# Four-layer graph network on one Trainium2 core: extra matmuls into an unused PSUM bank in five loops

## The chip, the cores and the metric

One core of a Trainium2 chip runs the whole program as one launch. The metric is the device time of one execution in microseconds (us); lower is better. PE is TensorE, DVE VectorE, ACT ScalarE, POOL GpSimd, SP SyncE.

## The reference

The graph has 3125 nodes with 128 numbers each and 100,000 edges, sorted by destination. Four layers follow one another, each ending in a residual and a layer norm:

```python
x = layernorm(x + L0(x))   # mean of x[dst] summed at src, then two 128x128 layers with relu
x = layernorm(x + L1(x))   # attention: q[dst] . (k[src] + e), softmax per dst, sum of weighted (v[src] + e), then gelu layers
x = layernorm(x + L2(x))   # (x + 3 * sum over edges of w * x[src_of_edge]) / 4
x = layernorm(x + L3(x))   # 18 relation matrices; messages of both directions summed at dst and at src
```

All numbers are float32.

## The kernel before

Edges are cut into tiles of 128, nodes into 25 blocks of 128. A (tile, block) couple that holds at least one edge of the block is a *pair*; there are 816 pairs, padded. A sum over edges is, for a pair, one 128x128 matmul of a 0/1 matrix ("hot", made by DVE by comparing locations with a row of column numbers) with 128 rows. Five loops matter here. In all of them POOL issues one indirect DMA for each of the 816 pairs, from the software queue.

- `send_rows` (L515 matmul, L501 hot matrix, L530 copy to SBUF, L562 indirect DMA). A step is four pairs; six steps ("ways") make a round, 34 rounds, 204 steps. SP loads the locations, DVE makes the hot matrix, PE multiplies it with rows of `x` that are picked by block number, ACT copies the product, POOL scatters it to DRAM. A way is used again after PE, ACT and the scatter have finished with it.
- `scores` (L1161 transpose, L1165 q matmuls, L1169 edge-feature matmul, L1077 indirect gather, L1122 and L1128 to L1135 on DVE, L1061 index copy). A step is four pairs, four ways, 51 rounds, 204 steps. PE transposes the edge features, ACT copies them, PE makes q (four 128-wide matmuls) and the feature product (one 512-wide one). DVE then adds (L1128), multiplies and reduces. POOL copies the indices of the step after the current one before it gathers the current one, and waits for that step's DVE addition of the round before.
- `gather_sum`, called three times (tags g2, g3, g4; L731 indirect gather, L742 hot matrix, L763 matmuls). A group is eight pairs, six ways, 17 rounds, 102 groups for each call. POOL's instructions are written out, and from the second round on it waits for `summed` of the way; so does DVE before it makes the way's hot matrix. PE waits for the hot matrices and the gathered rows, runs the eight matmuls, which add up in PSUM banks 0 to 6, and the last one increments `summed`.

TensorE's program in each of these loops first reads the block numbers of the step or group into registers, then waits, then runs its matmuls. Bank 7 of PSUM isn't used in them: `gather_sum` holds 25 x 128 columns, `send_rows` banks 0 to 5, `scores` banks 0 to 5. Nothing in them writes `S["ident"]` or the first block rows of `S["x"]`.

Other stages: sorting and tables (to about 523 us), `first_sum` (1724 to 2203), `weigh_values` (3789 to 4227), `messages` (5516 to 5633) and small ones between. They aren't touched.

Of the kernel before, what the change touches and what calls it, by code (L numbers as in the profile page):

```python
# [52 lines left out]
BANK = 512  # L53
# [408 lines left out]
                last.then_inc(turned, 1)  # L462


def send_rows(nc, S, dram):


# [4 lines left out]
    with ExitStack() as stack:  # L472
# [8 lines left out]
        ps = S["ps"]  # L481
        block = stack.enter_context(nc.Block())

        @block.sync
        def _(sp):
            with sp.Fori(0, WHOLE) as i:
                for q in range(WAYS):
                    sp.wait_ge(heated[q], i + 1)
                    sp.dma_start(locb[:, q, :], dram["loc"][bass.ds(i * (WAYS * STEP) + q * STEP, STEP), :]
                                 .rearrange("(a k) e -> a (k e)", a=1).to_broadcast([P, STEP * P])).then_inc(placed[q], 16)  # L490
# [12 lines left out]
        @block.tensor  # L503
        def _(pe):
            for q in range(WAYS):
                pe.sem_inc(picked[q], 1)
            with pe.Fori(0, WHOLE) as i:
                for q in range(WAYS):
                    _, cols = nc.values_load_multi_w_load_instructions(
                        S["dst_steps"][0:1, bass.ds(i * (WAYS * STEP) + q * STEP + PAIR_COLS, STEP)], engines=[mybir.EngineType.PE],  # L510
                        min_val=0, max_val=(BLOCKS - 1) * D, skip_runtime_bounds_check_because="block numbers are counts of blocks")
                    pe.wait_ge(heated[q], i + 2)
                    pe.wait_ge(laid[q], i * 2 + 1)
                    for j in range(STEP):
                        last = pe.matmul(ps[:, q * BANK + j * P:q * BANK + (j + 1) * P], hot_t[:, q, j * P:(j + 1) * P],  # L515
                                         S["x"][:, bass.ds(cols[j], D)], start=True, stop=True)
                    last.then_inc(picked[q], 1)
# [176 lines left out]
def load_columns(nc, S, eng, name, table, start):  # L694

    base = table * PAIR_COLS
    limits = [(BLOCKS - 1) * AW, (BLOCKS - 1) * D, (TILES - 1) * P]
    _, values = nc.values_load_multi_w_load_instructions(
        S[name + "_steps"][0:1, bass.ds(start + base, GROUP)], engines=[eng], min_val=0, max_val=limits[table],
        skip_runtime_bounds_check_because="counts of blocks and tiles, capped when they were made")  # L700
    return values


def gather_sum(nc, S, tag, name, table, index, weight=None, fresh=True):


    width, WAYS = D, 6
    WHOLE = PAIRS_PAD // (WAYS * GROUP)
    with ExitStack() as stack:
        m = Memory(nc, stack)  # L710
        got = m.sb(tag + "_got", [P, WAYS, GROUP, D])
        hot = m.sb(tag + "_hot", [P, WAYS, GROUP, P])
        landed, summed, heated = ([m.sem(f"{tag}_{n}{q}") for q in range(WAYS)] for n in (
            "landed", "summed", "hot"))
        hot_order, cleared = m.sem(tag + "_order"), m.sem(tag + "_cleared")
        loc, ps = S[name + "_loc"], S["ps"]
        block = stack.enter_context(nc.Block())

        def start_of(i, q):
            return i * (WAYS * GROUP) + q * GROUP  # L720

        @block.gpsimd
        def _(pool):
            for i in range(WHOLE):
                for q in range(WAYS):
                    if i:
                        pool.wait_ge(summed[q], i + 1)
                        pool.nop(nofuse=True)
                    for j in range(GROUP):
                        c = i * (WAYS * GROUP) + q * GROUP + j  # L730
                        pool.indirect_dma_start(out=got[:, q, j, :], out_offset=None, in_=table,  # L731
                                                in_offset=bass.IndirectOffsetOnAxis(ap=index[:, c:c + 1], axis=0)).then_inc(landed[q], 16)

        @block.vector
        def _(dve):
            if fresh:
                dve.memset(ps[:, 0:BLOCKS * D], 0.0).then_inc(cleared, 1)
            with dve.Fori(0, WHOLE) as i:
                for q in range(WAYS):
                    start = start_of(i, q)  # L740
                    dve.wait_ge(summed[q], i + 1)
                    one = dve.tensor_tensor(hot[:, q], S["col"][:, :].unsqueeze(1).to_broadcast([P, GROUP, P]),  # L742
                                            loc[:, bass.ds(start, GROUP)].unsqueeze(2).to_broadcast([P, GROUP, P]), ALU.is_equal)
                    if weight is not None:
                        one.then_inc(hot_order, 1)
                        dve.wait_ge(hot_order, i * WAYS + q + 1)
                        one = dve.tensor_tensor(hot[:, q], hot[:, q],
                                                weight[:, bass.ds(start, GROUP)].unsqueeze(2).to_broadcast([P, GROUP, P]), ALU.mult)
                    one.then_inc(heated[q], 1)

        @block.tensor
        def _(pe):
            for q in range(WAYS):
                pe.sem_inc(summed[q], 1)
            if fresh:
                pe.wait_ge(cleared, 1)
            with pe.Fori(0, WHOLE) as i:
                for q in range(WAYS):
                    columns = load_columns(nc, S, mybir.EngineType.PE, name, 1, start_of(i, q))
                    pe.wait_ge(heated[q], i + 1)  # L760
                    pe.wait_ge(landed[q], (i + 1) * (16 * GROUP))
                    for j in range(GROUP):
                        last = pe.matmul(ps[:, bass.ds(columns[j], width)], hot[:, q, j, :], got[:, q, j, 0:width],  # L763
                                         start=False, stop=True, skip_group_check=True)
                    last.then_inc(summed[q], 1)
            for q in range(WAYS):
                pe.wait_ge(summed[q], WHOLE + 1)
# [250 lines left out]
def scores(nc, S, dram):  # L1018
# [6 lines left out]
    with ExitStack() as stack:  # L1025
# [13 lines left out]
        ps = S["ps"]  # L1039
        block = stack.enter_context(nc.Block())  # L1040

        def qe(q):
            return ps[:, (q % 2) * 2 * BANK:(q % 2) * 2 * BANK + STEP * D]

        def feat(q):
            return ps[:, (q % 2) * 2 * BANK + BANK:(q % 2) * 2 * BANK + BANK + STEP * D]

        def turn(q):
            return ps[:, (4 + q % 2) * BANK:(4 + q % 2) * BANK + P]

        def before_last(eng, sems, q, i):

            if q < 2:
                eng.wait_ge(sems[q + 2], i + 1)
            else:
                eng.wait_ge(sems[q - 2], i + 2)
# [91 lines left out]
        @block.tensor  # L1148
        def _(pe):
            for q in range(WAYS):  # L1150
                pe.sem_inc(turned[q], 1)
                pe.sem_inc(product[q], 1)
            with pe.Fori(0, WHOLE) as i:
                for q in range(WAYS):
                    start = i * (WAYS * STEP) + q * STEP
                    _, cols = nc.values_load_multi_w_load_instructions(
                        S["dst_steps"][0:1, bass.ds(start + PAIR_COLS, STEP)], engines=[mybir.EngineType.PE], min_val=0,
                        max_val=(BLOCKS - 1) * D, skip_runtime_bounds_check_because="block numbers are counts of blocks")
                    pe.wait_ge(featured[q], (i + 1) * (16 * STEP))
                    before_last(pe, kept, q, i)  # L1160
                    pe.transpose(turn(q), attr[:, q, :], S["ident"][:, :]).then_inc(turned[q], 1)  # L1161
                    before_last(pe, scored, q, i)
                    pe.wait_ge(heated[q], i + 2)
                    for j in range(STEP):
                        pe.matmul(qe(q)[:, j * D:(j + 1) * D], hot_t[:, q, j * P:(j + 1) * P],  # L1165
                                  S["q"][:, bass.ds(cols[j], D)], start=True, stop=True)
                    pe.wait_ge(kept[q], i + 2)

                    pe.matmul(feat(q), attr_t[:, q % 2, :], S["w_e"][:, :], start=True, stop=True).then_inc(product[q], 1)  # L1169
# [463 lines left out]
```

## Time and profile before

| | us |
|---|---|
| three timed runs | 8021.37, 8027.81, 8035.16 |
| their median | 8027.81 |
| the profiled execution's own time | 8034.51 |
| its span | 8032.7 |
| `send_rows`, with what lies around it (523 to 1720) | 1197 |
| `scores` (2330 to 3672) | 1342 |
| g2, g3, g4 | 1173, 1185, 1184 |
| mean granted TensorE clock | 0.652 of full speed |

The profiled execution lies within the spread of the timed ones. The share of busy time of an engine counts its working instructions alone; waiting for a semaphore, register work and the issue of DMAs are not in it. A float32 matmul of the program shows as two LDWEIGHTS and two MATMUL records.

### The profile page before, as it was taken

Reading aid. Unit: us, or ns where it says so; the run is one execution under the profiler, and the core shown is the slowest. Engines: PE = TensorE matmul, PEld = TensorE weight load, DVE = VectorE, ACT = ScalarE, POOL = GpSimd, SP = SyncE. Lnnn points to the kernel's source line nnn. Section 1 sums busy time; section 2 is a strip of 40 time slices with the busy share of each in tenths; the row PEclk is TensorE's granted clock in tenths of the full one; section 3 lists DMA queues with packets and bytes.
Section 4 is the critical chain, followed back from the end, with each engine's and each line's share of the span. In section 5 each row is a group of like instructions: output and inputs, shape, how many; then the busy total and the mean of one; then the engine's idle time right before and its main releaser. Section 6 shows DMA issues by size and latency. Waiting matters only on the chain. (4 is left out here: it accounts for less than half of the span.)

```text
span 8032.7 us, 65229 instructions
## 1 busy us (share of the span) xinstructions
PE 2904.5 (36%) x12802; PEld 2351.3 (29%) x12803; DVE 2420.6 (30%) x4511; ACT 334.4 (4%) x878; POOL 4435.6 (55%) x5226
## 2 busy tenths in 40 slices
PE   0023333336644444442663333326333333233332
PEld 0012222235522222222552222223222222222222
DVE  2630000037734444445774122214111110011111
ACT  0001111100000000001001000000000000000000
POOL 0027777742226666662444666761666666776665
PEclk9985555567767777776885555557565555555555
DMA  2113223234426666664441111113211111111111
GB/s 87 26 57 95 85 90 93 88 83 116 105 78 170 172 172 170 171 169 115 122 121 33 47 44 47 46 45 148 66 45 45 45 45 43 47 46 45 45 45 46
DMA packets 688109, 674.55 MB, mean 84 GB/s; under 512 B 216326, under 2 KB 550142, under 8 KB 684346
## 3 DMA queue, kind: packets, MB, share of 16 engines
q0 software_dynamic: 144176, 323.21, 13.8%
q1 hardware_dynamic: 377036, 256.76, 11.6%
q10 hardware_dynamic: 166848, 94.11, 4.1%
q14 instruction: 41, 0.34, 0.0%
q8 instruction: 8, 0.13, 0.0%
HBM read 524.45 MB, written 164.31 MB: 86 GB/s over the span
## 5 line engine op out<-in xcount | busy, mean ns | idle before, releaser
L763 PE MATMUL ps<-g_got,g_hot 128*128 128x128 f32 x4896 | 1100.5, 383 | 2458.9 <-issue 1369.6
L763 PEld LDWEIGHTS ps<-g_got,g_hot 128*128 128x128 f32 x4896 | 986.1, 289 | 2573.5 <-issue 2572.8
L731 POOL DMA_INDIRECT g_got<-y,d_msg x816 | 820.2, 1005 | 526.4 <-issue 246.0
L731 POOL DMA_INDIRECT g_got<-x,s_dst x816 | 804.9, 986 | 443.3 <-issue 243.0
L731 POOL DMA_INDIRECT g_got<-y,s_msg x816 | 815.2, 999 | 369.3 <-issue 247.4
L562 POOL DMA_INDIRECT msg<-sr_pay,sr_place x816 | 801.8, 983 | 323.2 <-issue 290.7
L1077 POOL DMA_INDIRECT sc_kv<-kv,sc_cur x816 | 786.6, 964 | 264.9 <-issue 256.5
L742 DVE TENSOR_TENSOR g_hot<-col,src_loc 128x1024 f32<-128x1024 f32 x204 | 247.5, 1224 | 1922.5 <-remote 1100.4
L515 PE MATMUL ps<-x_rows,sr_hotT 128*128 x1632 | 382.7, 360 | 803.7 <-issue 745.1
L515 PEld LDWEIGHTS ps<-x_rows,sr_hotT 128*128 128x128 f32 x1632 | 319.2, 261 | 865.9 <-issue 864.6
L1165 PE MATMUL ps<-q,sc_hotT 128*128 x1632 | 299.3, 341 | 557.1 <-issue 401.2
L1165 PEld LDWEIGHTS ps<-q,sc_hotT 128*128 128x128 f32 x1632 | 266.2, 247 | 612.4 <-issue 602.6
L1128 DVE TENSOR_TENSOR sc_kve<-sc_kv,ps 128x1024 f32<-128x1024 f32 x204 | 249.1, 1221 | 642.9 <-remote 431.4
L742 DVE TENSOR_TENSOR g_hot<-col,dst_loc 128x1024 f32<-128x1024 f32 x102 | 122.6, 1224 | 1033.1 <-remote 559.0
L501 DVE TENSOR_SCALAR sr_hotT<-sr_locb,part 128x512 f32<-128x512 f32 x204 | 97.1, 504 | 1021.2 <-remote 927.1
L1338 POOL TENSOR_TENSOR wv_pv<-wv_ve,alpha_cols 128x1024 f32<-128x1024 f32 x102 | 212.9, 2088 | 340.4 <-PE ps L1395 218.6
L690 PE MATMUL ps<-fs_got,fs_hot 128*128 128x129 f32 x1632 | 310.4, 352 | 222.2 <-DVEq L666 160.8
L690 PEld LDWEIGHTS ps<-fs_got,fs_hot 128*128 128x128 f32 x1632 | 272.4, 253 | 261.5 <-issue 158.2
L1169 PE MATMUL ps<-w_e,sc_attrT 128*128 128x512 f32 x408 | 274.1, 760 | 181.1 <-issue 113.2
L1395 PE MATMUL ps<-wv_pv,wv_hot 128*128 128x132 f32 x1632 | 272.7, 335 | 180.2 <-DVEq L1380 164.1
L1395 PEld LDWEIGHTS ps<-wv_pv,wv_hot 128*128 128x128 f32 x1632 | 249.8, 238 | 203.1 <-issue 187.1
L626 POOL CAST s_dst<-fs_got 128x4 f32 x204 | 48.2, 236 | 379.6 <-DMA fs_got<-msg 379.6
(238 smaller groups left out, 2975.4 us busy)
## 6 DMA issues: line engine op xcount, KB each, us to landing
sr_locb<-loc SPq DMA_DIRECT2D x204, 256.0 KB
sc_locb<-loc SPq DMA_DIRECT2D x204, 256.0 KB
ve<-sc_kve ACTq DMA_DIRECT2D x204, 256.0 KB
wv_ve<-ve SPq DMA_DIRECT2D x102, 512.0 KB, 3.9
y<-ms_y SPq DMA_DIRECT2D x25, 1152.0 KB, 4.2
fs_got<-msg ACTq DMA_DIRECT2D x408, 66.5 KB, 1.9
fs_got<-msg SPq DMA_DIRECT2D x408, 66.5 KB, 1.9
msg<-sr_pay,sr_place POOLq DMA_INDIRECT x816
```

The source lines that it names most:

```text
L515: last = pe.matmul(ps[:, q * BANK + j * P:q * BANK + (j + 1) * P], hot_t[:, q, j * P:(j + 1) * P], S["x"][:, bass.ds(cols[j], D)], start=T ...
L562: pool.indirect_dma_start(out=dram["msg"], out_offset=bass.IndirectOffsetOnAxis(ap=place[:, c:c + 1], axis=0), in_=pay[:, q, j, :], in_off ...
L690: last = pe.matmul(part, hot[:, q, j, :], got[:, q, j, 0:width], start=True, stop=True)
L731: pool.indirect_dma_start(out=got[:, q, j, :], out_offset=None, in_=table, in_offset=bass.IndirectOffsetOnAxis(ap=index[:, c:c + 1], axis= ...
L742: one = dve.tensor_tensor(hot[:, q], S["col"][:, :].unsqueeze(1).to_broadcast([P, GROUP, P]), loc[:, bass.ds(start, GROUP)].unsqueeze(2).t ...
L763: last = pe.matmul(ps[:, bass.ds(columns[j], width)], hot[:, q, j, :], got[:, q, j, 0:width], start=False, stop=True, skip_group_check=True)
L1077: pool.indirect_dma_start(out=kv[:, q, j, :], out_offset=None, in_=dram["kv"], in_offset=bass.IndirectOffsetOnAxis(ap=cur[:, c:c + 1], axi ...
L1128: dve.tensor_tensor(kve[:, q].rearrange("p k (a d) -> p k a d", a=2), kv[:, q].rearrange("p k (a d) -> p k a d", a=2), feat(q).rearrange(" ...
L1165: pe.matmul(qe(q)[:, j * D:(j + 1) * D], hot_t[:, q, j * P:(j + 1) * P], S["q"][:, bass.ds(cols[j], D)], start=True, stop=True)
L1169: pe.matmul(feat(q), attr_t[:, q % 2, :], S["w_e"][:, :], start=True, stop=True).then_inc(product[q], 1)
L1338: pool.tensor_tensor(pv[:, h, :, 0:D].rearrange("p k (a c) -> p k a c", c=HEAD), ve[:, h].rearrange("p k (a c) -> p k a c", c=HEAD), S["al ...
L1395: last = pe.matmul(part, hot[:, h, j, :], pv[:, h, j, :], start=True, stop=True)
```

## The change

A helper issues matmuls that nobody reads: the identity as the stationary matrix, the first 512 columns of `x` as the moving one, bank 7 as the target. It is called with 6 in each group of `gather_sum`, with 3 in each step of `send_rows` and of `scores`, each time after the block numbers are read and before TensorE's waits for that group or step. The extra matmuls wait for nothing and increment nothing. No result of the kernel changes.

```diff
+def keep_running(pe, S, count):
+    for _ in range(count):
+        pe.matmul(S["ps"][:, 7 * BANK:8 * BANK], S["ident"][:, :], S["x"][:, 0:BANK], start=True, stop=True)
...
@@ send_rows, TensorE
                         min_val=0, max_val=(BLOCKS - 1) * D, skip_runtime_bounds_check_because="block numbers are counts of blocks")
+                    keep_running(pe, S, 3)
                     pe.wait_ge(heated[q], i + 2)
                     pe.wait_ge(laid[q], i * 2 + 1)
@@ gather_sum, TensorE
                     columns = load_columns(nc, S, mybir.EngineType.PE, name, 1, start_of(i, q))
+                    keep_running(pe, S, 6)
                     pe.wait_ge(heated[q], i + 1)
                     pe.wait_ge(landed[q], (i + 1) * (16 * GROUP))
@@ scores, TensorE
                         max_val=(BLOCKS - 1) * D, skip_runtime_bounds_check_because="block numbers are counts of blocks")
+                    keep_running(pe, S, 3)
                     pe.wait_ge(featured[q], (i + 1) * (16 * STEP))
                     before_last(pe, kept, q, i)
```

## Rows read from the trace of the kernel before

**Rows 1.** The page, part 2: granted clock in 40 slices.
```profile
PEclk9985555567767777776885555557565555555555
```
**Rows 2.** Windows: stretch, length, busy us of PE, PEld, DVE, ACT, POOL; clock, DMA, GB/s.
```profile
523.00:1720.00 1197.00, 382.73 (x1632) 319.24 (x1632) 100.10 (x206) 184.91 (x440) 843.26 (x1019) 0.56 0.29 89
...
2330.00:3672.00 1342.00, 581.65 (x2244) 368.37 (x2244) 632.86 (x815) 56.53 (x204) 825.22 (x1021) 0.72 0.63 169
...
4307.00:5480.00 1173.00, 365.16 (x1627) 325.49 (x1628) 248.01 (x205) 0.00 (x0) 804.87 (x816) 0.56 0.15 46
...
5639.00:6824.00 1185.00, 368.60 (x1632) 331.18 (x1632) 125.28 (x103) 0.00 (x0) 820.21 (x816) 0.57 0.16 45
6825.00:8009.00 1184.00, 365.95 (x1632) 328.83 (x1632) 122.30 (x102) 0.00 (x0) 815.23 (x816) 0.57 0.16 45
```
**Rows 3.** Groups by line: busy us, mean ns, idle before, releasers.
```profile
L731 POOL DMA_INDIRECT g_got<-y,s_msg x816 | 815.2, 999 | 369.3 <-issue 247.4 <-remote 113.2 <-ACTq L709 8.8
...
L562 POOL DMA_INDIRECT msg<-sr_pay,sr_place x816 | 801.8, 983 | 323.2 <-issue 290.7 <-ACT sr_pay L530 28.6 <-POOL sr_place L540 3.6
...
L515 PE MATMUL ps<-x_rows,sr_hotT 128*128 x1632 | 382.7, 360 | 803.7 <-issue 745.1 <-DVE sr_hotT L501 39.8 <-ACT sr_pay L530 10.8
...
L1509 PE MATMUL ps<-ms_w,ms_xT 128*128 128x512 f32 x200 | 99.2, 643 | 4.4 <-ACT ms_xT L1491 4.4
```
**Rows 4.** Line L763 alone: TensorE's instructions, ns least/median/most.
```profile
L763 PE MATMUL ps<-g_got,g_hot x4896: 269/421/581, 4323.6 to 8007.6; 128*128 128x128 f32 x196
L763 PEldq FUSED_REGOPS  x2448: 37/37/43, 4323.5 to 8005.0; - x189
```
**Rows 5.** Timeline of PE in g4, one cycle: start, length, what, idle before.
```profile
7032.28 8.03 PE L763 MATMUL ps<-g_got,g_hot 128*128 128x128 f32 x55 [0.33 <-issue]
...
7058.17 3.78 PE L763 MATMUL ps<-g_got,g_hot 128*128 128x128 f32 x16 [6.53 <-DMA g_got<-y,s_msg]
7068.12 3.78 PE L763 MATMUL ps<-g_got,g_hot 128*128 128x128 f32 x16 [6.17 <-DMA g_got<-y,s_msg]
...
7090.49 0.37 PE L763 MATMUL ps<-g_got,g_hot 128*128 128x128 f32 x1 [0.93 <-issue]
7094.02 0.37 PE L763 MATMUL ps<-g_got,g_hot 128*128 128x128 f32 x1 [3.15 <-issue]
7096.13 0.37 PE L763 MATMUL ps<-g_got,g_hot 128*128 128x128 f32 x1 [1.74 <-issue]
```
**Rows 6.** Timeline of DVE in the same cycle.
```profile
7073.12 1.23 DVE L742 TENSOR_TENSOR g_hot<-col,src_loc 128x1024 f32<-128x1024 f32 x1 [20.01 <-remote]
7117.24 1.22 DVE L742 TENSOR_TENSOR g_hot<-col,src_loc 128x1024 f32<-128x1024 f32 x1 [42.89 <-remote]
```
**Rows 7.** Timeline of POOL at the end of that cycle.
```profile
7127.08 0.95 POOL L731 DMA_INDIRECT g_got<-y,s_msg  x1 [0.30 <-issue]
7137.55 1.42 POOL L731 DMA_INDIRECT g_got<-y,s_msg  x1 [9.52 <-remote]
```
**Rows 8.** Windows: in g4 while TensorE crawls, and in scores while a product is late.
```profile
7090.00:7136.00 46.00, 6.91 (x19) 5.47 (x19) 1.22 (x1) 0.00 (x0) 27.98 (x30) 0.50 0.14 43
...
2620.00:2635.00 15.00, 3.85 (x17) 1.95 (x15) 4.36 (x6) 0.55 (x2) 10.00 (x13) 0.80 0.65 175
```
**Rows 9.** Timeline of PE in one round of scores.
```profile
2613.82 1.84 PE L1169 MATMUL ps<-w_e,sc_attrT 128*128 128x512 f32 x2
...
2621.37 1.13 PE L1169 MATMUL ps<-w_e,sc_attrT 128*128 128x512 f32 x2 [1.07 <-issue]
...
2622.44 1.06 PE L1165 MATMUL ps<-q,sc_hotT 128*128 x8
2624.79 1.13 PE L1169 MATMUL ps<-w_e,sc_attrT 128*128 128x512 f32 x2 [1.29 <-issue]
...
2638.70 1.64 PE L1165 MATMUL ps<-q,sc_hotT 128*128 x6 [11.91 <-issue]
```
**Rows 10.** Timeline of DVE, then of POOL, in that round.
```profile
2635.18 1.22 DVE L1128 TENSOR_TENSOR sc_kve<-sc_kv,ps 128x1024 f32<-128x1024 f32 x1 [9.82 <-remote]
...
2636.61 0.18 POOL L1061 COPY sc_cur<-d_src 128x4 int32 x1 [3.85 <-DVE sc_kve L1128]
```

## The prediction

> **What bounds the kernel now.** I read the page's clock slices first: TensorE is granted half speed, 0.5, in nearly all slices of `send_rows` and of the three row-gather sums [rows 1]. The windows by stage then say that the five loops of the change take 1197, 1342, 1173, 1185 and 1184 us, three quarters of the run, and that POOL is the only engine that is busy for two thirds of each [rows 2]. The groups by line give POOL's own pace: in g4 an indirect DMA is 999 ns of work and 247.4/816 = 0.30 us of issue, so about 1.3 us as a mean, and 0.95 + 0.30 = 1.25 us when undisturbed [rows 3, 7]. A group of eight is thus 10.0 us, and 102 groups 1020 us. The stage takes 1184. What is lost is in the same row: 113.2 us of "remote" waits, POOL waiting for `summed`, and the rest is the start, the end and the slightly longer DMAs.
>
> Why does POOL wait, with six ways and TensorE busy for a third of the stage? The timeline of one cycle of g4 shows it. At first TensorE takes a group whenever its rows land: 16 records in 3.78 us, every 10 us, starting at 7058.17 and at 7068.12. From 7090 on it crawls: single records 3.53 and 2.11 us apart, five and three times 0.70 us, with nothing that it waits for ("issue") [rows 5]. In 46 us it gets through 19 matmul records, 1.2 groups [rows 8]. The crawl ends when POOL has stopped: POOL's last DMA is at 7127.08, the next at 7137.55 [rows 7].
>
> The crawl is not the first sign. The group that TensorE ends at 7058.17 + 3.78 = 7061.95 is what DVE, idle and with nothing else to do, waits for; DVE starts at 7073.12, 11 us late. The next ends at 7071.90 and is seen at 7117.24, 45 us late [rows 5, 6]. So what TensorE sends out (its increments, and whatever leaves with every instruction) gets into a backlog, which grows while TensorE still runs at pace; when it is full, each further instruction waits for a place. 45 us at 0.70 us are about 64 entries. That there is such a queue is my inference; the lateness and the beat are rows. `scores` has the same thing in small: the product of the fourth step is done at 2624.79 + 1.13 = 2625.92, DVE adds it at 2635.18, 9.3 us late, and only then do TensorE's next q matmuls (11.91 us idle) and POOL's next index copy (3.85 us idle) go on [rows 9, 10]. `first_sum` and `weigh_values`, where POOL issues no indirect DMA, show no such beat. It is therefore tied to POOL's stream of indirect DMAs, and it costs each of the five loops the time between POOL's pace and the stage.
>
> **The change part by part.** Nothing is removed or moved; no wait and no DMA is added. Each call adds TensorE work ahead of the group's waits.
>
> *Price of one extra matmul.* The nearest are the 512-wide float32 matmuls of `messages`: 200 records, two for each matmul, 99.2 us, so 0.99 us at a mostly full clock [rows 3]. At half clock the feature product took 1.84 us [rows 9]. Six are 5.9 us warm and 11.0 cold; three are 3.0 and 5.5.
>
> *Row-gather sums.* A group's own matmuls take 3.78 us cold; in the fast stretch 55 records took 8.03 us, 2.3 us for 16 [rows 5]. Cold, 11.0 + 3.8 = 14.8 us would be above POOL's 10.0; but then TensorE never rests, and I take the full clock: 5.9 + 2.3 = 8.2 us. In steady state this lies beside POOL's 10.0 us and costs nothing. Two covers shrink, though. First, the catch-up: after a stop TensorE now runs 55 records, over three groups, in 8 us, and gives POOL and DVE their ways back; with the extras three groups take 25 us, for TensorE does the extras of the groups that are already there too. Second, the count of instructions: a group has 4896/306 = 16 matmuls, as many weight loads and 2448/306 = 8 register operations, 40 in all [rows 4]; six extras add 24. If the backlog counts instructions, at 10/0.70 = 14 leaving for each group it grows by 50 a group and not by 26, and is full after 1.3 groups, not 2.5. In the crawl 46 us brought 19 + 19 + 10 instructions, 0.96 us for each, so 24 more are 23 us for a group caught in it. Bounds: below 0 (all of it in TensorE's idle time); above, eleven crawls as now, 1.2 groups each, 23 us: 11 x 1.2 x 23 = 304 us a call. Between: the cycle, now about nine groups (102 groups, eleven stops), shrinks to about five, so twenty stops at the present 113.2/11 = 10.3 us are 206 in place of 113, +93; and I add 2 us at each stop for the slower way back, +40. I take +130 for each call, +390.
>
> *Scores.* The extras ahead of the first step fall into TensorE's 11.91 us of idleness. Those of the other three are in the chain from one DVE addition to the next: that step now is 3.4 us (2621.37 to 2624.79 [rows 9]), of which 1.1 + 1.1 and a short transpose are TensorE's; with 3.0 more it is 5.5. POOL needs one of these additions for each 4 x 1.25 + 0.2 = 5.2 us [rows 7, 10], so only 0.3 x 3 = 1 us of a round is directly exposed; the rounds after a rest start cold, at 5.5 for three extras, which adds up to 2.5. Lower bound 0, upper the whole stretch, 3 x 2.1 = 6.3 us for each of 51 rounds, 321 us. I take 2.6 us, +133.
>
> *Sending rows.* 204 steps in 1197 us are 5.87 us each; POOL alone needs 4 x (0.98 + 0.36) + 0.2 = 5.6 [rows 2, 3]. TensorE's step is 1632/204 = 8 records of 360 ns that overlap, about 2 us; with three extras 5 us warm and 7.5 cold. The "issue" idleness of 745.1 us says that the crawl fills most of this stage already [rows 3], so here the cover is thinnest. Lower bound 0; upper, twelve more instructions at 0.96 us in about a third of the steps, 68 x 11.5 = 782 us. A stop comes about every 50 us in the trace's pattern, 24 of them; I price each at 7 us more, +170, near the lower end because POOL waited for ACT only 28.6 us so far.
>
> *Sum.* 390 + 133 + 170 = +693. The profiled execution took 8034.5 us, 1.8 more than its span; 8728. Its time is 6.7 above the median of the runs, so 8720 for the median.
>
> *A rule weighed.* Rows: the granted clock is 0.56 in the sums and 0.72 in `scores` [rows 2]; yet in 2620 to 2635, with 0.80 granted, the product was 9.3 us late [rows 8 to 10]. The Trainium skill, "TensorE: Matmul & The Clock Gate", section "Why this matters for your kernels", says that idle gaps between bursts bring TensorE back to the half rate and that it should be kept busy; by it the real matmuls of a group fall from 3.8 to 2.3 us, which is off the path here and changes the sum by nothing, unless the crawl goes with it (first rival). The Trainium skill, "Advanced Engine Details and Errata", section "Clock Domains", speaks against that: the sequencer of TensorE is not behind the clock gate. By that rule a higher clock leaves the 0.70 us beat as it is, with which the row at 0.80 agrees.
>
> **The rivals.**
>
> *Keeping TensorE occupied ends the crawl (faster).* For: it appears only in stages with long TensorE pauses beside POOL's DMAs, and in the crawl the clock is 0.50 throughout [rows 8]. Against: the late product at clock 0.80. It is one mechanism, with its place in what leaves TensorE, and decides if lateness stays under the lead of six ways, 60 us less one group in flight. Price: each call falls to 1020 + 20, saving 422 us over three; scores loses its 3.85 us and about 0.5 more a round, 220; sending about 30. 8034 - 672 = 7362; half of it 7700.
>
> *Nothing happens.* TensorE's idleness covers all and the backlog counts something other than matmuls. For: 8.2 < 10.0. Against: scores' chain. Time 8028.
>
> *TensorE becomes the bound in the crawl.* 64 instructions at 0.96 us are 61 us a group; if a third of the groups were caught, 34 x 23 = 782 more a call, and with the upper ends elsewhere over 10,000. For: nothing lets TensorE catch up in 8 us any more. Against: the crawl ends when POOL stops, which limits it.
>
> **How the numbers follow.** The likeliest, slower by a few per cent, 0.60, with its own range 8150 (only scores and a part of sending) to 9400 (most of the upper bounds, 912 + 321 of sums and scores with sending at 170). TensorE bound in the crawl 0.10. Nothing 0.08. Faster 0.22, half of it under 7650. Leaving out that half and the top half of the crawl case, 7650 to 9500 holds 8 in 10. About 16 us, 0.2%, is what a measurement of this kernel can tell from no change. Faster 0.22, same 0.08, slower 0.70; time 8720.
>
> **What would show it.** In the windows of g2 to g4: stages of about 1300 us, clock near 1.0 outside the crawl, more and earlier stops of POOL (over fifteen waits of about 10 us a call), DVE starts that lag TensorE's group ends by tens of us. In scores: 2.6 us a round more, TensorE's idle gap shorter. In sending: POOL waiting for `sr_pay` by a few hundred us. I am wrong if single records 0.70 us apart have gone, or if POOL's waits in the sums fall: then the backlog is fed by TensorE's pauses and not by its instructions. I am wrong in size if TensorE stays at half clock, for then 14.8 us a group bound the sums at 1500 us each.

## The result and the profile after

The change makes the kernel slower by 2.69%: 8240.63 us against 8024.85 (medians), ratio 1.0269, 95% interval 1.0252 to 1.0287. The forecast was slower, which holds, as do the range and the likeliest case's own (8150 to 9400). The time, 8720 us, doesn't: 216 us were lost, not 693. The profiled execution has a span of 8236.3 us, 203.6 more than before.

The page's clock slices after, the windows of the five stages (columns as in [rows 2], mean clock third from the end) and the groups by line:

```profile
PEclk9998888777778889886886887888788888788878
```
```profile
523.00:1757.00 1234.00, 878.19 (x2853) 481.81 (x2851) 97.08 (x203) 181.71 (x440) 839.92 (x1019) 0.81 0.28 86
2375.00:3760.00 1385.00, 1051.11 (x3467) 556.37 (x3465) 626.67 (x814) 56.53 (x204) 824.53 (x1021) 0.88 0.61 164
4395.00:5613.00 1218.00, 851.53 (x2856) 480.25 (x2856) 250.19 (x205) 0.00 (x0) 827.34 (x816) 0.80 0.15 44
5764.00:6993.00 1229.00, 854.81 (x2855) 487.46 (x2856) 126.84 (x103) 0.00 (x0) 816.18 (x816) 0.81 0.17 44
6994.00:8213.00 1219.00, 853.54 (x2856) 485.13 (x2856) 124.22 (x103) 0.00 (x0) 813.02 (x816) 0.81 0.17 44
```
```profile
L469 PE MATMUL ps<-x_rows,ident 128*128 128x512 f32 x6120 | 3102.7, 645 | 367.3 <-issue 333.0 <-DVE ps L745 25.3
...
L772 PE MATMUL ps<-g_got,g_hot 128*128 128x128 f32 x4896 | 834.0, 307 | 924.0 <-issue 897.5 <-DMA g_got<-y,d_msg 10.3 <-DMA g_got<-y,s_msg 6.6
...
L739 POOL DMA_INDIRECT g_got<-y,s_msg x816 | 813.0, 996 | 416.1 <-issue 238.4 <-remote 140.2 <-ACTq L717 36.5
...
L570 POOL DMA_INDIRECT msg<-sr_pay,sr_place x816 | 797.7, 978 | 394.3 <-issue 343.2 <-ACT sr_pay L538 46.0 <-POOL sr_place L548 4.8
```

Lines have moved: L731 is now L739, L763 L772, L562 L570. Against [rows 2 and 3]: the clock in the sums rose from 0.57 to 0.81, an own matmul record of the sums takes 307 ns as a mean, against a median of 421 [rows 4], an extra costs 3102.7/3060 = 1.01 us. TensorE gained speed, and the stages still grew.

POOL's waits by line (total us, times, longest), before and then after:

```profile
POOL g_got L731 <- remote: 269.9, 38, 10.8
...
POOL sc_cur L1061 <- DVE sc_kve L1128: 218.6, 84, 7.4
```
```profile
POOL g_got L739 <- remote: 306.7, 81, 7.6
...
POOL sc_cur L1070 <- DVE sc_kve L1137: 256.7, 80, 6.2
```

This is the row that decides the size: POOL waits for `summed` twice as often, 81 times for 38, but 3.8 us each where it was 7.1.

From the first and last indirect DMA of POOL in each stage and the end of TensorE's last group, the 203.6 us divide so: row sending +43, scores +42; inside the sums +28, +16, +17; and +16, +29, +18 behind them, from POOL's last DMA to TensorE's end (the "tail", below). What lies between the stages adds up to some 6 us less. One crawl of g4 after, timelines of PE and of POOL and two windows:

```profile
7122.48 2.71 PE L469 MATMUL ps<-x_rows,ident 128*128 128x512 f32 x5
7126.48 1.11 PE L469 MATMUL ps<-x_rows,ident 128*128 128x512 f32 x2 [1.29 <-issue]
7127.89 0.59 PE L469 MATMUL ps<-x_rows,ident 128*128 128x512 f32 x1 [0.30 <-issue]
7129.29 1.31 PE L469 MATMUL ps<-x_rows,ident 128*128 128x512 f32 x2 [0.82 <-issue]
7132.12 0.59 PE L469 MATMUL ps<-x_rows,ident 128*128 128x512 f32 x1 [1.51 <-issue]
...
7137.05 0.37 PE L772 MATMUL ps<-g_got,g_hot 128*128 128x128 f32 x1 [1.72 <-issue]
7139.16 0.37 PE L772 MATMUL ps<-g_got,g_hot 128*128 128x128 f32 x1 [1.74 <-issue]
...
7144.75 2.51 PE L772 MATMUL ps<-g_got,g_hot 128*128 128x128 f32 x11 [1.03 <-issue]
7147.05 6.95 PE L469 MATMUL ps<-x_rows,ident 128*128 128x512 f32 x12
```
```profile
7139.85 0.95 POOL L739 DMA_INDIRECT g_got<-y,s_msg  x1 [0.30 <-issue]
7145.61 1.42 POOL L739 DMA_INDIRECT g_got<-y,s_msg  x1 [4.81 <-remote]
```
```profile
7126.00:7145.00 19.00, 6.59 (x14) 3.20 (x15) 0.02 (x1) 0.00 (x0) 11.32 (x12) 0.69 0.17 45
7145.00:7169.00 24.00, 23.14 (x79) 12.86 (x78) 3.66 (x3) 0.00 (x0) 17.91 (x19) 0.89 0.17 47
```

The 0.70 us beat, single records that start a multiple of 0.70 us apart with no wait, is still there (1.41 us between starts, 2.11 between others). It doesn't depend on the clock: the four starts from 7126.48 to 7132.12 are 1.41, 1.40 and 2.83 us apart at a granted clock of 1.00 (7126 to 7133), and those at 7137.05 and 7139.16 are 2.11 apart at 0.50 (7135 to 7145). The crawl lasts 19 us, not 46, POOL's stop 4.81, not 9.52 [rows 7]. Then TensorE works without a pause for 24 us, almost three groups with their extras, and is back in the crawl: 27 intervals between the 28 stops of g4 span 1095 us, 41 us each; before, eleven stops span 1051 us, 105 us each.

The tail, last POOL DMA and last group of g4 after; before they stood at 7999.84 and 8004.29 + 3.78:

```profile
8186.18 0.94 POOL L739 DMA_INDIRECT g_got<-y,s_msg  x1 [0.30 <-issue]
```
```profile
8205.11 5.32 PE L469 MATMUL ps<-x_rows,ident 128*128 128x512 f32 x12
8210.26 1.95 PE L772 MATMUL ps<-g_got,g_hot 128*128 128x128 f32 x16
```

### The profile page after: what moved, and what is told of

It is laid out like the page before. It is cut to its first block and busy times, and to the rows that moved or that the text cites. A ratio compares the mean times of both kernels' runs of the same rounds, so it can differ in the third digit from the quotient of the medians.

```text
span 8236.3 us, 77469 instructions
## 1 busy us (share of the span) xinstructions
PE 5324.2 (65%) x18922; PEld 3166.2 (38%) x18923; DVE 2419.8 (29%) x4511; ACT 330.8 (4%) x878; POOL 4450.6 (54%) x5226
## 5 line engine op out<-in xcount | busy, mean ns | idle before, releaser
L469 PE MATMUL ps<-x_rows,ident 128*128 128x512 f32 x6120 | 3102.7, 645 | 367.3 <-issue 333.0
L469 PEld LDWEIGHTS ps<-x_rows,ident 128*128 128x128 f32 x6120 | 1237.0, 210 | 1847.2 <-issue 1845.1
L772 PE MATMUL ps<-g_got,g_hot 128*128 128x128 f32 x4896 | 834.0, 307 | 924.0 <-issue 897.5
L772 PEld LDWEIGHTS ps<-g_got,g_hot 128*128 128x128 f32 x4896 | 749.5, 217 | 1176.0 <-issue 1175.8
L739 POOL DMA_INDIRECT g_got<-y,d_msg x816 | 816.2, 1000 | 556.4 <-issue 236.0
L739 POOL DMA_INDIRECT g_got<-x,s_dst x816 | 827.3, 1014 | 448.8 <-issue 241.1
L739 POOL DMA_INDIRECT g_got<-y,s_msg x816 | 813.0, 996 | 416.1 <-issue 238.4
L570 POOL DMA_INDIRECT msg<-sr_pay,sr_place x816 | 797.7, 978 | 394.3 <-issue 343.2
L523 PE MATMUL ps<-x_rows,sr_hotT 128*128 x1632 | 274.2, 298 | 206.1 <-issue 204.9
L523 PEld LDWEIGHTS ps<-x_rows,sr_hotT 128*128 128x128 f32 x1632 | 250.9, 209 | 341.0 <-issue 340.9
L1175 PE MATMUL ps<-q,sc_hotT 128*128 x1632 | 230.3, 286 | 84.0 <-issue 79.4
```

The source lines that it names most:

```text
L469: pe.matmul(S["ps"][:, 7 * BANK:8 * BANK], S["ident"][:, :], S["x"][:, 0:BANK], start=True, stop=True)
L570: pool.indirect_dma_start(out=dram["msg"], out_offset=bass.IndirectOffsetOnAxis(ap=place[:, c:c + 1], axis=0), in_=pay[:, q, j, :], in_off ...
```

## The experiments

The runs went to several chips. On some, the kernel before takes 7976 to 8031 us (medians), as in the trace above ("with the beat"). On two others it takes 7251 and 7252 us, and nothing crawls. Each run is compared with the kernel before that was timed beside it on its own chip, as a ratio with its 95% interval. Between groups of runs the level itself moves: one chip took 7976 us for the kernel before, and 8031 half an hour later. So differences between runs of different groups are less sure than their intervals say, and the change itself was timed with the beat in one group alone. "Stops" are gaps of over 3 us between the starts of POOL's DMAs in the sums, with the time by which they exceed 1.25 us; before they are 40 with 324 us, after 82 with 376.

### With the beat: what the cost goes by

**Narrow extras.** The same count, a quarter of the columns.
```diff
-        pe.matmul(S["ps"][:, 7 * BANK:8 * BANK], S["ident"][:, :], S["x"][:, 0:BANK], start=True, stop=True)
+        pe.matmul(S["ps"][:, 7 * BANK:7 * BANK + P], S["ident"][:, :], S["x"][:, 0:P], start=True, stop=True)
```


> All extras are kept in number and place, but 128 columns wide instead of 512: the same 24 and 12 TensorE instructions a group and step, about a quarter of the array time. Theory I (the number of TensorE instructions feeds the backlog): nearly the whole loss stays, +150 to +216 us over before. Theory A (the array time of the extras is what costs: the catch-up after a crawl and the end of each stage are slower): most of it goes, 0 to +70 us over before.

8152.83 against 8019.54 us, 1.0153 (1.0133 to 1.0173): +133 of 216, between the two expectations. By stage, against runs on the same chip whose row sending and scores have no extras, row sending loses 38 to 39 us and scores 46 to 60 (the change: 43 and 42). There it is nearly all the count. The sums lose 48 us with their tails, against the run with no-operations below; in the change they lose 125, so there the wide columns add more.

**No-operations in their place,** 24 a group and 12 a step.
```diff
-    for _ in range(count):
-        pe.matmul(...)
+    for _ in range(4 * count):
+        pe.nop(nofuse=True)
```


> The extras are replaced by as many no-operations (24 a group, 12 a step), no array time at all. Theory I, if any instruction of TensorE's program counts: +100 to +216 us. Theory A: within 20 us of before. If narrow matmuls cost and no-operations don't, then what counts is what passes through the array's queue.

8017.68, 0.9998 (0.9988 to 1.0007). So many instructions in TensorE's stream cost nothing by themselves, and what feeds the beat isn't just any instruction. No-operations leave no record in the trace, a matmul of the program leaves four.

**Extras in the sums alone** (the two calls with 3 removed).


> Extras in the three row-gather sums alone. From the stage times of the two traces (+45, +44 and +34 us for g2, g3 and g4, of +204) both theories give +115 to +130 us over before if the stages are independent; my prediction had +390 here.

8134.38, 1.0137 (1.0120 to 1.0154), +115: over half of the change.

**Half of the group's own matmuls left out** of the kernel before; the sums then cover only four of each eight pairs.
```diff
-                    for j in range(GROUP):
+                    for j in range(GROUP // 2):
```


> The kernel before, without extras, with the second half of the eight matmuls of each group of the row-gather sums left out (so the sums lack half of the pairs): 16 matmul and weight-load records and 4 register operations fewer a group, all DMAs as before. Theory I: the backlog needs about twice as long to fill, POOL's stops fall from 11 to 17 a sum to half or fewer, 100 to 300 us less in all. Theory A: array time isn't what POOL waits for before, so within 30 us of before.

7947.64, 0.9915 (0.9898 to 0.9932), -72, again between the two expectations. Stops fell to 34 only, but with 189 us. Fewer matmuls make it faster, with the clock at 0.50 in the sums (0.57 before).

**Last round of each sum without extras.**
```diff
-            with pe.Fori(0, WHOLE) as i:
...
+            with pe.Fori(0, WHOLE - 1) as i:
+                one_round(i, True)
+            one_round(WHOLE - 1, False)
```


> The changed kernel, but the last of the 17 rounds of each row-gather sum runs without extras. In the two traces TensorE ends 16, 29 and 18 us later after POOL's last gather than before the change, 63 us in all. Theory T (these ends are TensorE working off a debt of extras that nothing hides any more): 40 to 65 us less than the changed kernel. Theory I (only the beat during POOL's stream matters): under 15 us less, since a crawl in the last round is as likely as before.

8136.18 against 7976.31, 1.0197 (1.0177 to 1.0218). That is 0.72% or 58 us less than the change loses, across two groups of runs. The tails are 9.6, 7.2 and 7.7 us; in the change they were 28.5, 36.2 and 26.0. The tail is a cost of its own: whatever groups TensorE is behind when POOL ends, it then does with six extras each.

**Twelve ways in place of six,** no extras. The 102 groups are then eight rounds of twelve and one of six, which the lines left out take care of.
```diff
-    width, WAYS = D, 6
+    width, WAYS = D, 12
...
```


> The kernel before, without extras, with twelve ways in the row-gather sums instead of six (two rounds' worth of buffers, same work, same order). Theory I (a crawl lasts until POOL has used up its lead and stops; one stop costs the same however long the lead is): stops fall from 11 to 17 a sum to 5 to 8, 100 to 180 us less in all. If POOL instead waits because TensorE is too slow on average, doubling the buffers saves only the first few us, under 30.

7983.39, 1.0010 (0.9999 to 1.0020): the expected gain isn't there. The waits:
```profile
POOL g_got L732 <- remote: 217.2, 21, 17.9
```
The waits came half as often and took 10.3 us each. All stops together are 35 with 296 us, and the tails are 17, 27 and 25 us; on the same chip, the run with extras in row sending alone (below) leaves the sums as before, with 40 stops, 323 us and 27 us of tails in all. More lead makes fewer and longer stops, and what is gained in them is given back at the end.

**Gathers of the sums as plain DMAs from SP,** of consecutive rows and not the indexed ones, so that the sums add up other data.
```diff
-        @block.gpsimd
+        @block.sync
...
-                        pool.indirect_dma_start(out=got[:, q, j, :], ...).then_inc(landed[q], 16)
+                        sp.dma_start(got[:, q, j, :], table[k * P:(k + 1) * P, :]).then_inc(landed[q], 16)
```


> The kernel before, without extras, with the gathers of the three sums replaced by as many plain DMAs of 128 consecutive rows each, issued by SP (so the sums are over other rows): same bytes, same TensorE program, no software-made DMAs. Theory I says that the beat needs POOL's indirect DMAs: no single records 0.70 us apart in these stages, increments seen at once, and each sum at what TensorE or SP allow, under 500 us. If the beat comes from TensorE's own instruction count alone, it shows here as well, and more often, since the pace is higher.

One execution: 5637.96 us, with the first of the sums done in 393 us. TensorE's idleness ahead of the same matmuls:
```profile
L760 PE MATMUL ps<-g_got,g_hot 128*128 128x128 f32 x4896 | 718.7, 307 | 493.1 <-DMA g_got<-y 320.9 <-DMA g_got<-x 154.0 <-DVE g_hot L744 17.3
```
No "issue" is among its causes, where the after row has it first. The chip had the beat in this very execution: row sending, which still has POOL's indirect DMAs, took 1168 us from its first to its last, where a chip without the beat takes 1057. So on a chip that has the beat it goes with POOL's indirect DMAs.

**Row sending alone.**


> Extras in the row sending alone. Stages independent: +35 to +50 us over before (+43 between the traces), against my +170.

8018.19 against 7976.31, 1.0051 (1.0033 to 1.0069), +42, which is also what the stage grew in the change.

**Twice the narrow extras,** 12 and 6. The first two times it came to a chip without the beat, the third to one with it.
```diff
-                    keep_running(pe, S, 6)
+                    keep_running(pe, S, 12)
```


> The extras are 128 columns wide, as in the narrow run, and twice as many: twelve in each group of the sums, six in each step of row sending and scores. Theory: what the three stages of sending, scores and sums lose goes by the number of instructions that TensorE sends out while POOL streams indirect DMAs. Narrow extras cost 133 us for six and three; twice the count gives twice that, 266 us (ratio 1.033, 1.028 to 1.040), with sending at about 1250 us and scores at about 1410. Rival, a threshold: only having extras at all moves the rounds (their place in front of the waits), so the second half adds little, under 170 us in all (1.021 or less). Second rival, the backlog of the prediction: twice as many stops at a full price, over 400 us (above 1.05).

> Twelve narrow extras in each group of the sums, six in each step of row sending and scores. On a chip with the beat, theory: linear in the count of instructions, twice the 133 us of the narrow run, 1.028 to 1.040. Rival, a threshold: 1.021 or less. Rival, the prediction's backlog at its own price: above 1.05. On a chip without the beat: within 0.3%.

> Twelve narrow extras in each group of the sums, six in each step of row sending and scores. On a chip with the beat, theory: linear in the count, twice the 133 us of the narrow run, 1.028 to 1.040; rival, a threshold: 1.021 or less. On a chip without the beat: 1.001 to 1.003 once more.

With the beat: 8268.73 against 8030.61, 1.0293 (1.0278 to 1.0309), +238 for double the count that gave +133. The total is nearly linear, and the prediction's own price (above 1.05) is out. There are 90 stops with 366 us. The stages are not linear one by one. Against the run with three wide extras in the sums, on the same chip and untouched in the other two stages, row sending loses 69 us (38 to 39 with half the count) and scores 46 (46 to 60). The remaining 123 us are in the sums (48). So, as far as runs on two chips can be compared, the second half of the extras adds nothing in scores, as the threshold rival had it, and more than the first in the sums. That the total comes out nearly double is in part luck. Without the beat: 1.0017 (1.0008 to 1.0026) and 1.0025 (1.0014 to 1.0035), 12 and 16 us.

**Three wide extras in the sums alone.**
```diff
-                    keep_running(pe, S, 6)
+                    keep_running(pe, S, 3)
```


> Extras in the sums alone, three in each group in place of six. Theory: POOL's wait in a sum follows the mean pace of TensorE, so half the instructions and half the array time cost half of what six do: 0.7% (0.5 to 0.9%), some 55 us. Rival: the cost comes from the catch-up after a stop, where it matters only once extras and own matmuls together exceed POOL's 10 us a group at half clock; three extras (5.5 + 3.8 = 9.3 us) stay below it and cost under 0.3%.

> Three extras in each group of the sums and nowhere else. On a chip with the beat: half of the 1.37% of six, 0.5 to 0.9%. Rival, the catch-up theory (it costs only where extras and own matmuls exceed 10 us a group at half clock; here 9.3): under 0.3%. On a chip without the beat: no change.

> Three wide extras in each group of the sums and nowhere else. On a chip with the beat: half of the 1.37% of six, 0.5 to 0.9%; rival, the cost starts where extras and own matmuls exceed POOL's 10 us a group: under 0.3%. On a chip without the beat: no change, within 0.15%.

With the beat: 8064.51, 1.0040 (1.0025 to 1.0055), +34, where six cost 115. The point lies between the two expectations; the cost per wide extra rises with their number, from 0.04 us for each of 918 to 0.06 for each of 1836. 55 stops with 323 us. Without the beat: 1.0002 and 1.0006.

**Scores alone.** Both times on a chip without the beat.


> Extras in the scores alone, three in each step. Theory: the three parts add up; all together gave 2.69%, the sums alone 1.37% and row sending alone 0.51%, so this part alone gives the rest, 0.6 to 0.8% (50 to 65 us), 45 of it inside the stage. Rival: the parts share a common cost and do not add up; then this run is within 0.3% of the kernel before.

> Three extras in each step of scores and nowhere else. On a chip with the beat: 0.5 to 0.8% slower (40 to 65 us), the part that is left of 2.69% after 1.37% for the sums and 0.51% for row sending. Rival: under 0.3%, so that the parts do not add up. On a chip without the beat: no change.

1.0000 (0.9991 to 1.0009) and 1.0004 (0.9995 to 1.0013). The share of scores with the beat is therefore known only from the stage's length (+42 us, 0.52%) and from the rest, 2.69 - 1.37 - 0.51 = 0.81%.

### Without the beat: what is left of the cost

In the first run of scores alone, row sending and sums are those of the kernel before. Its windows (row sending, scores, g2), the waits of POOL in the sums and the groups by line:

```profile
523.00:1594.00 1071.00, 410.94 (x1632) 354.91 (x1632) 102.44 (x205) 187.81 (x442) 837.74 (x1021) 0.51 0.38 100
2214.00:3268.00 1054.00, 947.75 (x3466) 511.75 (x3464) 612.15 (x813) 56.65 (x204) 829.52 (x1020) 0.99 0.83 215
3905.00:4962.00 1057.00, 377.57 (x1632) 354.81 (x1632) 252.10 (x205) 0.00 (x0) 800.03 (x816) 0.65 0.19 51
```
```profile
POOL g_got L738 <- issue: 745.0, 2445, 0.3
```
```profile
L770 PE MATMUL ps<-g_got,g_hot 128*128 128x128 f32 x4896 | 1148.1, 429 | 2033.7 <-DMA g_got<-x,s_dst 689.5 <-DMA g_got<-y,d_msg 675.8 <-DMA g_got<-y,s_msg 668.3
...
L738 POOL DMA_INDIRECT g_got<-x,s_dst x816 | 800.0, 980 | 334.4 <-issue 248.4 <-ACTq L716 86.0
```

Row sending takes 1071 us (1197 in [rows 2]) and a sum 1057 (1173), scores with three extras 1054, against 1342 before and without them. POOL never waits for `summed`, and 816 x (0.98 + 0.30) = 1045 us is nearly the whole of a sum, 1048 from its first indirect DMA to its last. TensorE is as idle as before and nearly as slow (0.51 to 0.66); it waits for rows, with no "issue". Idleness or a low clock thus doesn't by itself make the beat.

**The change again.**


> The change itself, once more, beside the next three runs. Theory: its cost exists only where the kernel before shows the beat of 0.70 us, so two outcomes are foreseen. On a chip where the kernel before takes about 8000 us: ratio 1.025 to 1.030. On a chip where it takes about 7250 us: within 0.3% of the kernel before, since double the count of narrow extras cost 0.17% there. Rival: on a quiet chip the array time of wide extras shows in the chain of scores (2 us a round, 100 us, 1.4%) though the narrow ones did not.

This chip had no beat: 7338.10 against 7251.18, 1.0121 (1.0105 to 1.0136), +87. "Within 0.3%" was wrong, and so was the rival, for scores took 1046 us from the first to the last indirect DMA, against 1048 in the run on this chip that has extras in the sums alone. Some 10 us are in row sending, the rest in the sums, in POOL's DMAs themselves:

```profile
L739 POOL DMA_INDIRECT g_got<-y,d_msg x816 | 826.4, 1013 | 414.1 <-issue 248.3 <-ACTq L717 165.8
L739 POOL DMA_INDIRECT g_got<-x,s_dst x816 | 835.6, 1024 | 334.9 <-issue 248.3 <-ACTq L717 86.6
```

The waits are the same to a microsecond, and the DMAs are 23 to 36 us longer for each call, together 85 us. Of the 2448, 139 take over 1.5 us, where the second run with scores alone has 8. One of them, and DVE's comparison beside it, on their timelines:

```profile
6731.44 0.95 POOL L739 DMA_INDIRECT g_got<-y,s_msg  x1 [0.30 <-issue]
...
6738.93 0.95 POOL L739 DMA_INDIRECT g_got<-y,s_msg  x1 [0.30 <-issue]
6740.18 1.96 POOL L739 DMA_INDIRECT g_got<-y,s_msg  x1 [0.30 <-issue]
```
```profile
6731.55 1.23 DVE L750 TENSOR_TENSOR g_hot<-col,src_loc 128x1024 f32<-128x1024 f32 x1 [10.12 <-PE ps L772]
6740.10 1.23 DVE L750 TENSOR_TENSOR g_hot<-col,src_loc 128x1024 f32<-128x1024 f32 x1 [7.33 <-PE ps L772]
```

The comparison started 0.08 us ahead of the DMA, which then took 1.01 us more. Where it began inside a DMA (6731.55, the DMA at 6731.44) that DMA kept 0.95, and the comparison its 1.23.

All DMAs of the sums bear this out. In this run 431 start while DVE works on a hot matrix (the comparison, or in one of the sums the multiplication behind it). Of these, 309 take over 1.0 us, and they end 0.82 us after the DVE operation (median). The 1877 with no such operation beside them take 0.944 us as a mean. What the 431 take above that is 163 us together. In the second run with scores alone 402 start so and take 79 us more, and the 1757 without one take 0.944 us as well. The difference, 84 us, is all that the DMAs are longer between these two runs. So the extra matmuls don't slow POOL's DMAs themselves; they move the moment at which TensorE's group ends and DVE starts, and more DMAs then start just behind a comparison.

The Trainium skill, "SBUF — State Buffer", section "SBUF: two separate sides", says that a DVE operation with two SBUF inputs and a GpSimd operation that reads SBUF exclude each other on a shared port pair: whichever starts first has it for the whole instruction, and the other waits. For the DMA behind the comparison the rows agree. The other way round they don't: 253 of these DVE operations start inside a DMA, and none of them is longer than 1.26 us.

**DVE shifted.** An unused tile is filled before the comparison.
```diff
                     dve.wait_ge(summed[q], i + 1)
+                    dve.memset(spare[:, q, :], 0.0)
```


> The change, and in the sums DVE fills an unused tile (128x512, some 0.3 to 0.6 us) after its wait and before it makes the hot matrix, so that the comparison starts that much later against POOL's steady 1.25 us beat of DMAs. On the chip without the beat, theory: 139 of the 2448 DMAs of the sums take 1.7 us or more in place of 0.95, because the comparison starts just ahead of them; shifted, their number changes, to under 70, and the time falls by 40 to 80 us against the change (ratio to the kernel before under 1.007 in place of 1.012). Rival: the extra matmuls slow POOL's DMAs themselves; then their number and the time stay, 1.011 to 1.013. On a chip with the beat: within 0.3% of the change, 1.024 to 1.030.

It came to a chip with the beat, so a shift was never tried without it; that the meeting of the engines is the cost there rests on the count above. But the run told something else. It took 8223.01 against 8030.61, 1.0236 (1.0222 to 1.0250), the same as the change or a little less, though

```profile
L740 POOL DMA_INDIRECT g_got<-y,d_msg x816 | 856.9, 1050 | 505.2 <-issue 243.5 <-ACTq L717 178.2 <-remote 82.9
L740 POOL DMA_INDIRECT g_got<-y,s_msg x816 | 854.8, 1048 | 355.2 <-issue 244.1 <-remote 82.8 <-ACTq L717 28.3
L740 POOL DMA_INDIRECT g_got<-x,s_dst x816 | 854.6, 1047 | 417.5 <-issue 244.2 <-ACTq L717 86.0 <-remote 44.8
```

POOL's DMAs became 110 us longer over the three sums than in the change (2566 against 2457), and its stops 142 us shorter in all (38 with 234). With the beat, POOL's waits are slack that its own work can fill, so the pace is set elsewhere. That it is set where TensorE's instructions leave it is my reading.

## Why the prediction was right in sign and wrong in size

**The bound: right with the beat.** The 0.70 us beat, tied to POOL's stream of indirect DMAs, is what a stage loses over POOL's own pace. The plain-DMA run and the chips without a beat show it from two sides; on the latter the kernel before is 720 to 780 us faster, while a POOL DMA there is as long within 3%. What the beat is was not settled. A backlog of entries that leave TensorE remains my inference, and that not all chips have it wasn't foreseen. The prediction fed the backlog with every instruction, register operations too; the no-operations, which cost nothing, don't bear that out.

**Price of an extra, 0.99 us warm: right,** 1.01 measured; and TensorE stayed warm enough, 0.81.

**"Twenty stops at the present 113.2/11 = 10.3 us ... +93": the step that failed.** The sums were put at +390 us and grew by 125. The number of stops was even too low (25, 29 and 28 in g2, g3 and g4), and the price, 376/82 = 4.6 us, less than half. A stop isn't an event of fixed length: over six kernels with the beat and a group's full sixteen own matmul records (before, after, narrow, double narrow, three wide, twelve ways) the count went from 35 to 90 and the total only from 296 to 376 us. In a seventh, shifted, it is 38 with 234, while POOL's own work grew by 110 us. The reading that fits all seven is that the total is the difference between POOL's pace and TensorE's mean pace in the beat, however it is cut; that mean pace was not measured by itself. What should have been priced is that difference: the stages grew by 28, 16 and 17 us inside, not by 130.

**"2 us at each stop for the slower way back", +40: wrong in place.** The way back does lengthen, to 24 us without a pause. But a cost at each stop doesn't show: inside the sums the three stages are only 61 us longer, for 82 stops in place of 40. The slower way back is paid once a call, in the tail, 63 us over three calls, which the prediction didn't have; the run without a last round of extras shows it.

**Scores, +133: the term mis-sized,** +42. POOL's wait for the addition rose by 38 us (218.6 to 256.7), 0.75 us a round for the 2.6 taken. On the chips without the beat three extras cost nothing there, so the chain that I thought exposed has its slack. With the beat narrow extras cost as much as wide ones there (46 to 60), so the width isn't what costs.

**Row sending, +170: mis-sized,** +43, again by stops at a price of their own, 24 x 7. Gaps of over 3 us between the starts of POOL's DMAs are 31 there before and 42 after; beyond 1.25 us each they hold 109 and 162 us. The wait for `sr_pay` rose only from 28.6 to 46.0; the loss shows as "issue", 290.7 to 343.2 us.

**The first rival, occupied TensorE ends the crawl: refuted.** The clock rose to 0.8 and the beat stayed; half of the matmuls left out made it faster with a colder TensorE (0.50 in the sums); and row sending without the beat runs at 0.51. In the crawl shown above the spacing is a multiple of 0.70 us at a granted clock of 1.00 and at 0.50 alike. The rule of the Trainium skill that the prediction named, "Advanced Engine Details and Errata", section "Clock Domains", a TensorE sequencer that isn't behind the clock gate, agrees with that.

**TensorE bound in the crawl, nothing: neither came.** On a chip without the beat the second comes nearly true for narrow extras (0.2%), but not for the change itself (1.2%).

Left open: what the beat is, why a wide extra costs more from the fourth on, why a second three narrow extras cost the scores nothing, and what differs between the chips.

## What to carry to other kernels

Beside a stream of indirect DMAs from POOL, count TensorE's matmuls, not only their time: on a chip with the beat 3060 matmuls that nobody waits for cost 133 us even when narrow, and warming the clock gave nothing back, since the clock wasn't the bound. Where two engines run at different mean paces, price the paces and the backlog at the end, not the number of stops. And look at more than one chip before a cost of this kind is called the kernel's.

## What the runs showed of the hardware

The same program takes 7244 to 7256 us on two chips (51 runs) and 7963 to 8042 on the others. Beside POOL's indirect DMAs a narrow extra matmul costs 0.04 us as a mean over these loops with the beat (133/3060, 238/6120) and 0.002 to 0.003 without it (12 to 16 us for 6120); no-operations cost nothing that can be measured (0.9998). An indirect DMA of POOL that starts 0.08 us behind a two-input comparison of DVE takes 1.96 us, not 0.95: it ends 0.82 us after the comparison. A comparison that starts inside the DMA is not lengthened.
